# Deformable convolution started before its pass count is known, with a TensorE loop body of eight tiles

## What is computed

```python
out = jax.nn.relu(batchnorm(conv2d(x, w1), g1, b1))
offsets = conv2d(out, w_off) + b_off[None, :, None, None]
out = batchnorm(deform_conv(out, offsets, w2), g2, b2)
return jax.nn.relu(out + x)

def deform_conv(x, offset, w):           # 9 taps, each moved by its own offset, bilinear
    px = rows + pn_x + off[..., :N];  py = cols + pn_y + off[..., N:]
    px = jnp.clip(px, 0, Hp - 1);     py = jnp.clip(py, 0, Wp - 1)
    xo = g_lt * gather(x0, y0) + g_rb * gather(x1, y1) + g_lb * gather(x0, y1) + g_rt * gather(x1, y0)
    return conv(xo, w, stride 3)
```

## Time and profile before

| what | us |
|---|---|
| median of 3 runs | 2418.48 (2417.71 to 2423.48) |
| the profiled execution, its own time | 2415.32 |
| span of that execution (first to last instruction) | 2413.5 |
| TensorE busy | 2262.6 (94%) |
| first transposition of the deformable stage starts | 1827.30 |
| `final` loads begin | 2368.56 |

### The profile page before, as it was taken

How to read it: one execution, slowest core, us unless ns; L and a number is a source line. 1 busy time by engine, 2 the same in 40 slices (tenths; PEclk the granted TensorE clock), 3 DMA queues, 4 the chain that set the end, 5 groups by cost and what they waited for, 6 DMA issues and landing times.

```text
span 2413.5 us, 73170 instructions
## 1 busy us (share of the span) xinstructions
PE 2262.6 (94%) x26669; PEld 1827.2 (76%) x26669; DVE 1806.1 (75%) x3885; ACT 1798.3 (75%) x2963; POOL 1438.8 (60%) x1095
## 2 busy tenths in 40 slices
PE   5999999999999999999999999699897999999992
PEld 3777777777767777777777777588566999999992
DVE  6778877778867777877777777587665878787875
ACT  5788888888878888888888888533565777776764
POOL 4669656666656666655666666674116666666650
PEclk9999999999999999999999999899998999999996
DMA  3978798978888878978877777773234433343427
GB/s 91 197 174 169 168 186 163 176 178 167 180 175 157 179 174 174 178 158 152 177 178 174 178 174 177 198 238 102 56 85 133 130 118 118 116 122 112 130 85 279
DMA packets 1048662, 378.62 MB, mean 157 GB/s; under 512 B 975344, under 2 KB 1035376, under 8 KB 1040240
## 3 DMA queue, kind: packets, MB, share of 16 engines
q1 hardware_dynamic: 1048432, 375.42, 66.7%
HBM read 98.76 MB, written 41.68 MB: 58 GB/s over the span
## 4 chain that ended last, share of the span: by engine, by line
PE 74%; POOL 11%; issue 7%; DVE 3%; DMA 3%; ACT 1%; SPq 0%; POOLq 0%; ACTq 0%; DVEq 0%
PE psum L1042 14%; PE psum L1043 14%; PE psum L1044 14%; POOL probs_split L367 9%; PE psum L1082 7%; PE psum L1084 7%; PE psum L1083 7%; PE psum L1225 5%; PE psum L1198 2%; DMA probsT_dma<-probs_split 2%; PE psum L1068 2%; PE psum L1206 1%; PE psum L1188 1%; DMA final<-x_scratch 1%; DVE neg_max L715 1%
## 5 line engine op out<-in xcount | busy, mean ns | idle before, releaser
L367 POOL TENSOR_TENSOR probs_split<-probs,probs_split 128x896 f16<-128x896 f32 x512 | 966.6, 1888 | 526.0 <-ACT probs_split L517 525.9
L715 DVE TENSOR_REDUCE neg_max<-psum 128x1 f32<-128x1024 f32 x512 | 626.3, 1223 | 307.4 <-PE psum L1044 304.8
L514 ACT ACTIVATE probs<-psum,exp_bias 128x1024 f32<-128x1024 f32 x512 | 570.6, 1114 | 184.2 <-DVE exp_bias L717 182.2
L1082 PE MATMUL psum<-vT_hi,probsT_dma 128*128 128x129 f16 x3584 | 637.6, 221 | 11.9 <-DMA probsT_dma<-probs_split 11.9
L1084 PE MATMUL psum<-vT_hi,probsT_dma 128*128 128x129 f16 x3584 | 637.4, 219 | 0.0
L1083 PE MATMUL psum<-vT_lo,probsT_dma 128*128 128x128 f16 x3584 | 637.2, 218 | 0.0
L517 ACT ACTIVATE probs_split<-probs 128x896 f16<-128x896 f32 x512 | 486.5, 950 | 24.6 <-DMA probsT_dma<-probs_split 2.1
L459 POOL TENSOR_TENSOR interp<-row_hats,col_hats 128x360 f32<-128x360 f32 x384 | 294.4, 795 | 200.0 <-PE psum L1225 195.1
L1042 PE MATMUL psum<-k_hi,q_hi 128*128 128x512 f16 x1024 | 388.4, 379 | 4.5 <-DVE q_lo L831 2.5
L1043 PE MATMUL psum<-k_lo,q_hi 128*128 128x512 f16 x1024 | 388.6, 379 | 0.0
L1044 PE MATMUL psum<-k_hi,q_lo 128*128 128x512 f16 x1024 | 388.6, 379 | 0.0
(11 more groups left out here) (177 smaller groups left out, 4897.6 us busy)
## 6 DMA issues: line engine op xcount, KB each, us to landing
xt_windows<-xt_scratch SPq DMA_DIRECT2D x192, 320.0 KB
xt_scratch<-zeros_f SPq DMA_DIRECT2D x28, 576.0 KB, 4.3
probsT_dma<-probs_split SPq DMA_TRANSPOSE x512, 3.4
x_residual<-x SPq DMA_DIRECT2D x128, 64.0 KB, 2.4
x_scratch<-x_out SPq DMA_DIRECT2D x128, 64.0 KB, 2.1
x_rows<-x_scratch SPq DMA_DIRECT2D x32, 256.0 KB, 3.4
xt_scratch<-xt_stage SPq DMA_DIRECT2D x128, 64.0 KB
final<-x_scratch SPq DMA_DIRECT2D x16, 512.0 KB, 10.1
```

Of the source, the lines that this page charges most:

```text
L367: po.tensor_tensor(PH[j][:, 1, :], P[:, j, 0:128 * DT[j]], PH[j][:, 0, :], ALU.subtract).then_inc(s["pl"], 1)
L514: act.activation(P[:, j, :], sc, ACT.Exp, bias=NB[:, par, j:j + 1]).then_inc(s["exp"], 1)
L715: ve.tensor_reduce(NM[:, par, j:j + 1], sc, AX.X, ALU.max, negate=True).then_inc(s["mx"], 1)
L1082: pe.matmul(dst, th, Vh[:, p, v, 0:129], start=n == 0, stop=False)
```

## The change

1. The stage doesn't wait for the pass count. Each engine starts with a register that holds 1 and runs the first pass; at the end of it the engine reads the count (`count_passes`). The shifts are reordered, so that pass 0 is the one with shift zero. Per partition maxima go to DRAM and come back as a row; SP does this between the windows of image 2 and those of image 3. VectorE makes the counts (three now) after its last loop, ahead of the last four steps. TensorE's transposition of the maxima is gone.
2. The first `distances` are made by GpSimd in the offset stage, in eight parts (`first_distances`), beside the chunks of image 2. The first `hats` are made by ScalarE beside the chunks 1, 3, 5 and 7 of image 3. For that the hats and windows lie where they don't overlap what the offset stage uses. ScalarE's `shift_of(0)` goes ahead of the offset stage. The last half image makes the distances and hats of a next pass.
3. TensorE's loop has a body of eight tiles: eight are written out ahead, fifteen iterations follow. It keeps `repeat`.
4. The loops of ScalarE, VectorE and GpSimd in conv1, in the offset stage and in the deformable stage turn from `repeat` into `Fori`.

The diff, cut to its core:

```diff
+        def count_passes(eng, n, regs):
+            after(eng, "fg", n * FLAG + FLAG)
+            eng.sem_inc(s_go, 1)
+            for r, (col, most) in regs:
+                eng.reg_mov(r, eng.value_load(CNT[0:1, col:col + 1], min_val=1, max_val=most))
 # SP
-            for i in range(2):
-                stored(sp, s_xs[i], B * NCH * 2)
-            after(sp, "l1", L1_FLAG)
-            ny = sp.value_load(CNT[0:1, 2:3], min_val=1, max_val=SY)
-            nx = sp.value_load(CNT[0:1, 3:4], min_val=1, max_val=SX)
...
+            sp.reg_mov(ry, 1)
+            sp.reg_mov(rx, 1)
+            with sp.Fori(0, ry) as iy_:
+                iy = sp.snap(iy_, min_val=0, max_val=SY - 1)
+                with sp.Fori(0, rx) as ix_:
+                    ix = sp.snap(ix_, min_val=0, max_val=SX - 1)
+                    sy = sp.snap((iy + SY // 2) % SY, min_val=0, max_val=SY - 1)
+                    sx = sp.snap((ix + SX // 2) % SX, min_val=0, max_val=SX - 1)
...
+                    def image_windows(b, last):
+                        for i in range(2):
+                            stored(sp, s_xs[i], b * (NCH * 2) + NCH * 2)
+                            sp.sem_inc(s_go, 1)
+                        for i in range(HH // TW):
+                            if i == HH // TW - 1 and not last:
+                                stored(sp, s_xs[0], b * (NCH * 2) + (NCH * 2 + TW))
+                                sp.sem_inc(s_go, 1)
+                            windows(b, i)
+                    with sp.Fori(0, B - 1) as b:
+                        image_windows(b, False)
+                    n = iy * SX + ix
+                    after(sp, "l1", L1_MAX)
+                    sp.dma_start(max_dram, SM[:, 28:29]).then_inc(s_fs, 16)
+                    sp.wait_ge(s_fs, n * 16 + 16)
+                    sp.dma_start(FLR[:, :], max_dram.rearrange("p a -> a p")).then_inc(s_fl, 16)
+                    image_windows(B - 1, True)
+                    count_passes(sp, n, ((ry, (1, SY)), (rx, (2, SX))))
 # GpSimd
+            def first_distances(k):
+                if k == 0:
+                    after(po, "fin", 2)
+                    after(po, "cv", B * NCH)
+                gs = slice(4 * (k % 4), 4 * (k % 4) + 4)
...
             for m in range(B * NCH):
                 after(po, "hA", m + 1)
                 po.memset(Y[:, m // NCH, 512 * (m % NCH):512 * (m % NCH) + 512], 0.0).then_inc(s["fz"], 1)
-            after(po, "l1", L1_FLAG)
-            npass = po.value_load(CNT[0:1, 0:1], min_val=1, max_val=PASSES)
+                if m in range(2 * NCH, 3 * NCH):
+                    first_distances(m - 2 * NCH)
...
+            after(po, "of", B * NCH)
+            after(po, "ot", B * NCH)
+            after(po, "xt", B * NCH)
...
-                with repeat(po, 0, NHALF // 2 - 1) as u:
+                with po.Fori(0, NHALF // 2 - 1) as u:
 # ScalarE
+            act.wait_ge(s_kl, 16)
+            shift_of(0)
+            def offset_image(b, rbs, first, hoist=False):
...
+                    if hoist and rb in (1, 3, 5, 7):
+                        hats(0, 0, rb // 2)
...
-            after(act, "l1", L1_FLAG)
-            after(act, "xe", B * NCH)
-            npass = act.value_load(CNT[0:1, 0:1], min_val=1, max_val=PASSES)
...
-                with repeat(act, 0, NHALF // 2 - 1) as u:
+                with act.Fori(0, NHALF // 2 - 1) as u:
 # VectorE
-                with repeat(ve, 1, NHALF) as h:
+                with ve.Fori(1, NHALF) as h:
                     half_image(h, range(HALF), False)
+                for step in range(FLAG):
+                    flag(step)
                 half_image(NHALF - 1, range(HALF, HALF + 4), False)
+                count_passes(ve, n, ((passes, (0, PASSES)),))
 # TensorE
-            after(pe, "l1", L1_MAX)
-            pe.transpose(PS[0:1, 6, 0:128], SM[:, 28:29], ident).then_inc(s["fl"], 1)
-            after(pe, "l1", L1_FLAG)
             after(pe, "xe", B * NCH)
-            npass = pe.value_load(CNT[0:1, 0:1], min_val=1, max_val=PASSES)
+            after(pe, "ocp", B * NCH)
...
-                half_image(0, range(HALF), True)
-                with repeat(pe, 1, NHALF) as h:
-                    half_image(h, range(HALF), False)
-                half_image(NHALF - 1, range(HALF, HALF + 2), False)
+                eight_tiles(0, range(8), True)
+                with repeat(pe, 1, GROUPS // 8) as h:
+                    eight_tiles(h, range(8), False)
+                eight_tiles(GROUPS // 8 - 1, range(8, 10), False)
+                count_passes(pe, n, ((passes, (0, PASSES)),))
```

More of the change, by code:

```diff
@@ L312, in _ @@
-            npass = sp.value_load(CNT[0:1, 0:1], min_val=1, max_val=PASSES)
[L313 to L324, removed]
+            ry, rx = sp.alloc_register("passes_y"), sp.alloc_register("passes_x")
@@ L462, in interp, with half_image @@
                 last.then_inc(s["pr"], 1)
-            with po.Fori(0, npass) as n:
-                def half_image(h, hb, last):
+            after(po, "of", B * NCH)
+            after(po, "ot", B * NCH)
+            after(po, "xt", B * NCH)
+            passes = po.alloc_register("passes")
+            po.reg_mov(passes, 1)
+            with po.Fori(0, passes) as n:
+                def half_image(h, hb, image):
                     hid = n * NHALF + h
@@ L469, in half_image @@
                         interp(hid * HALF + g, hb, g)
[L470 to L474, removed]
-                with repeat(po, 0, NHALF // 2 - 1) as u:
[L476 to L479, removed]
+                        if g == 5 and image is not None:
+                            after(po, "fin", image * FIN + 2)
+                        if g in (5, 8):
+                            distances(hid + 1, (h + 1) * HALF if image is not None else 0, 1 - hb, int(g == 8))
+                with po.Fori(0, NHALF // 2 - 1) as u:
+                    half_image(u * 2, 0, u)
+                    half_image(u * 2 + 1, 1, u + 1)
+                half_image(NHALF - 2, 0, B - 1)
+                half_image(NHALF - 1, 1, None)
+                count_passes(po, n, ((passes, (0, PASSES)),))
             after(po, "l1", L1_VAR2)
@@ L600, in offset_pixels, with hats, shift_of @@
                 act.activation(OFF[:, bass.ds(m * 4, 4), :], src, ACT.Copy).then_inc(s["ocp"], 1)
-            def offset_image(b, rbs, first):
+            def hats(hid, hb, step):
+                shift = SM[:, 32 + step % 2:33 + step % 2]
+                dst = (HX, HY)[step % 2][:, hb, :, :, :]
+                if step < 2:
+                    after(act, "hd", hid * 2 + (step + 1))
+                    act.activation(dst, dst, ACT.Abs, bias=shift).then_inc(s["hb"], 1)
+                else:
+                    after(act, "hb", hid * 2 + (step - 1))
+                    act.activation(dst, dst, ACT.Relu, scale=-1.0, bias=1.0).then_inc(s["hx"], 1)
+            def shift_of(n):
+                act.activation(SM[:, 32:34], CL[:, bass.ds(n * 2 + (K_SH - K_LO), 2)], ACT.Copy).then_inc(s["sh"], 1)
+                after(act, "sh", n + 1)
+            act.wait_ge(s_kl, 16)
+            shift_of(0)
+            def offset_image(b, rbs, first, hoist=False):
                 for rb in rbs:
@@ L643, in sampled @@
                 act.activation(dst, src, ACT.Copy).then_inc(s["xh"], 1)
[L645 to L655, removed]
+            passes = act.alloc_register("passes")
+            act.reg_mov(passes, 1)
+            with act.Fori(0, passes) as n_:
+                n = act.snap(n_, min_val=0, max_val=PASSES - 1)
                 def half_image(h, hb, first, last):
@@ L662, in half_image @@
                             interp_hi(q, g, i)
-                        if not last and g in (10, 11, 12, 13):
+                        if last and g == 9:
+                            shift_of(n + 1)
+                        if g in (10, 11, 12, 13):
                             hats(hid + 1, 1 - hb, g - 10)
@@ L892, in _ @@
             conv1_image(0, True)
-            with repeat(ve, 1, B) as b:
+            with ve.Fori(1, B) as b:
                 conv1_image(b, False)
@@ L997, in z_add, with flag @@
                 ve.tensor_tensor(yz, src, yz, ALU.add).then_inc(s["z"], 1)
-            with ve.Fori(0, npass) as n:
+            with ve.Fori(0, passes) as n:
+                def flag(step):
+                    if step == 0:
+                        ve.wait_ge(s_fl, n * 16 + 16)
+                        ins = ve.tensor_reduce(SM[0:1, 29:30], FLR[:, :], AX.X, ALU.max)
+                    elif step == 1:
+                        ins = ve.tensor_scalar(SM[0:1, 30:31], SM[0:1, 29:30], REACH, None, ALU.is_gt)
+                    else:
+                        ins = ve.scalar_tensor_tensor(CNT[0:1, :], CL[0:1, K_CA - K_LO:K_CB - K_LO], SM[0:1, 30:31],
+                                                      CL[0:1, K_CB - K_LO:K_SEL - K_LO], ALU.mult, ALU.add)
+                    ins.then_inc(s["fg"], 1)
```

(1 more changed line is left out.)

106 lines of the change are left out of this document (62 added, 44 removed).

## The result

| what | before | after |
|---|---|---|
| median of the runs side by side | 2420.09 (2417.71 to 2423.48) | 2383.14 of 4 runs (2381.59 to 2383.99) |
| span of the profiled execution | 2413.5 | 2382.2 |
| first transposition of the deformable stage | 1827.30 | 1812.05 |
| first sample | 1831.18 | 1818.60 |

The ratio is 0.9846, with a 95% interval of 0.9828 to 0.9863.

A forecast was written before the change was run, and what follows sets the result against it. TensorE was taken as the bound, losing time at its branches and at the seam. Terms summed to -30.7: 2415.3 to 2384.6, plus 3.2 for the median, say 2388; range 2378 to 2402, leaving out rivals A and B.

The forecast's parts named there:

- TensorE's branches: TensorE's deformable loop: a body of eight tiles stays in the engine, so slow branches back go; -22.7 us, bounds -22.7 and -19.7.
- Rival A: TensorE's deformable loop: the eight-tile body is fetched anew all the same at fourteen branches; +22.3, so 2441; chance 0.12.
- The seam: Between offset and deformable stage: sampling starts 11.9 us earlier, with the first window late next; bounds -15.4 and -9.
- The clock: TensorE's first samples after the seam: 4.5 us at half speed after the pause, +2.2 us, range 0 to 3.5.
- Hats in image 3: ScalarE in the offset stage: each hat delays a chunk by about 0.8; +2.2 us, bounds 0 and 6.05.
- `first_distances`: GpSimd's eight small subtractions in the offset stage fit its idle time; 0 us, bounds 0 and 3.
- Loops without hint: Loops losing their hint: ScalarE's two issue stalls may go, its long body may miss; -1 us, bounds -3.7 and +4.4.
- Rival B: Unhinted loops of the engines other than TensorE miss at their branches: 19 us in place of -1, so 2408; chance 0.08.

The follow-up runs named there:

- the first experiment: The kernel before with only TensorE's deformable loop changed, to a body of eight tiles: median 2391.19, ratio 0.9879, span 2390.9.
- the early windows: Changed kernel, ScalarE's deformable loop written out, TensorE's offset loop unhinted, plus SP issuing image 0's first two windows between the offset stage's last stores: 2379.07, ratio 0.9834.

## Why the prediction was right, point by point

**TensorE's branches, -22.7.** Right in mechanism: 216 ns, hidden, no tile made late by any of the fourteen. Right in size for the profiled executions: the span of the first experiment moved by 22.6. By the medians the body is worth 28 to 30. Rival A is out: 8 blocks don't stay, 6.9 do.

**The seam, -11.9.** The size was right (-11.5), the reason only half. SP's setup, estimated at 2 us, took 1.9; the first window landed at 1817.9, where 1819.3 was forecast, as the last store was 0.8 earlier and issue to landing took 7.7 us, not 8.2. But TensorE didn't wait for it: it fetched its own instructions until 1816.85, had its transpositions to finish, and sampled 0.7 us behind the window. Without the fetch it did wait for the window (the version with L1284 unhinted), and gained only 0.3. That hinted loops leave the next block out was a thought of the prediction for ScalarE; it wasn't applied to TensorE, which leaves the hinted loop L1284 just here.

**The clock, +2.2.** +1.2: the low level ended at 1820.96, 2.4 us into the samples, as this row shows (clock third from the right), where 4.5 was taken:

```profile
1810.75:1820.90 10.15, 6.69 (x38) 5.94 (x39) 4.37 (x9) 3.48 (x7) 7.72 (x11) 0.50 0.64 183
```

**Hats in image 3, +2.2.** +1.1: the chunks with a hat took 3.52, 3.76 and 3.43 us, so 0.33, 0.57 and 0.24 for each, where 0.8 was taken: a hat of 1.5 us less the 0.7 of the stall at 1742 that was absorbed. The hats took 1.49, 1.73 and 1.40 us, so 1.2 of each was absorbed. What failed is carrying the 0.7 over from the stall; why more is absorbed here wasn't tested.

**`first_distances`, 0.** Right: `padded_lo` on VectorE took 1.18 to 1.29 us beside the subtractions, where it took 0.71 without them (at 1701.61), and the chunks stayed at 3.19.

**Loops without hint, -1.** This term failed: it came to +2.9. ScalarE's two stalls went as thought (-1.5 at 1742, -1.7 at the end of its loop). Its two branches missed, which the prediction had only as the end of its range, at +4.4; they cost 3.9 + 2.2 = 6.1. The step that went wrong is the row chosen for the branch: 45 ns is that of L1301, whose body is short. The duration of the branch on ScalarE shows nothing of it; it is 50 and 45 ns here as well, and 4.84 and 3.97 us stand behind it as issue. Rival B's mechanism is real, but only in the engine with the long body: VectorE and GpSimd show no such stall.

**What the sum didn't have.** The tile behind the one that starts at 1852.7 was 0.96 late in before, and isn't now. The offset stage's third chunk came 0.9 later; the clock's low level reached 8.8 us into the stage in the trace of after (1699.54 to 1708.3), 6.9 in that of before (1701.07 to 1707.9). In the other traces too the chunk was late where that level reached furthest (8.6 us in two of them). The work ahead of it, which the change hardly touches, ended 1.5 us earlier. In the traces of the kernels here the first chunk began between 1697.2 and 1703.2, in one at 1706.9: this is what one profiled execution can't tell, and agreement to 1 to 3 us between a sum and a span is partly luck. That -30.7 met -31.3 hides one term that was 4 off and several of about 1 that went the other way.

**Span and median.** The median fell by 37, the span by 31: the runs of before vary more, and its profiled one, 2415.3, was below its median. The prediction's sum gave 2384.6 for a profiled execution, and 2383.99 was measured. It then added the 3.2 us by which before's median lay above its profiled run. That step failed: the changed kernel's runs lie within 2.4 us of each other, and its median, 2383.14, is 0.9 below the profiled one. Most of the 4.9 us between 2388 and 2383.14 is this, and not a term of the sum.

## What to carry to other kernels

Count a hot loop's instructions, and look at the engine's instruction queue over the loop. Packets in step with the iterations mean that the body is fetched anew; here each branch back then waited, although it was hinted, and halving the body cost nothing. Where the body stays with the hint and without it, leave the hint out: on TensorE it moved a fetch to a place where it was waited for. For ScalarE's long body, writing it out beat both kinds of loop. Don't carry the distance between one profiled run and its median over to a kernel whose fetches are gone. And before starting something earlier, ask what is queued behind it: the early windows held up the stores, and the early hats met a wait that was there anyway.

## What the runs showed of the hardware

- TensorE kept a loop of 816 + 816 matmuls and weight loads with its waits and had branches of 216 ns; with 960 + 960 and the hint they took 2.4 to 5.5 us. Where between the two the limit lies wasn't measured.
- Behind a hinted loop an engine fetched what came next: 2.06 us on TensorE behind L1284 (2.38 and 5.08 us at the same place in two other runs), 4.91 us on ScalarE 38 us behind L734. Without the hint TensorE's wait is gone, at no cost at its branches (213 ns and 214 ns), and ScalarE's long body stood for 4.84 and 3.97 us at its branches.
- The kernel whose branches fetch varied more: 2404.96 to 2416.43 in ten runs with sixteen tiles, 2381.59 to 2383.99 in four with eight, otherwise the same kernel.
- VectorE's `padded_lo` took 1.18 to 1.29 us instead of 0.71 while GpSimd subtracted beside it, and held nothing up.
